# Attention and FFN on one core: the preparation of keys, values and weights rebuilt

## The reference

```python
kv = latent_kv @ Wkv_expand.T                      # ctx (8, 64, 256), Wkv (2048, 256)
k, v = jnp.split(kv, 2, axis=-1)
qp = q @ Wq.T                                      # q = layernorm(x), x (8, 1024, 1024)
scores = einsum(qh, kh) / sqrt(64)                 # 16 heads of 64, 64 keys; causal mask
attn = softmax(where(causal, scores, min))
x = x + einsum(attn, vh) @ Wout.T
# then, on layernorm(x): both sides rounded to fp8 (e4m3) by one scale each,
x = x + scaled_mm(x_fp8, w_fp8.T)
```

## Time and profile before

| | us |
|---|---|
| median of 3 runs | 1797.81 |
| lowest and highest run | 1797.55, 1800.09 |
| the profiled execution, its own time | 1799.89 |
| its span, first to last instruction | 1798.1 |
| TensorE busy | 1744.1 (97%) |
| VectorE busy | 1343.6 (75%) |
| ScalarE busy | 689.0 (38%) |
| GpSimd busy | 185.3 (10%) |
| HBM read, written | 119.28 MB, 71.30 MB |

### The profile page before, as it was taken

The page is one execution under the profiler, slowest core; times in us unless marked ns, Lnnn a source line. Parts: engine busy times, 40 slices in busy tenths (PEclk is TensorE's granted clock), DMA queues, the critical chain, the costliest instruction groups (busy, mean ns, idle before and its releaser), DMA issues.

```text
span 1798.1 us, 26754 instructions
## 1 busy us (share of the span) xinstructions
PE 1744.1 (97%) x10698; PEld 842.0 (47%) x10730; DVE 1343.6 (75%) x1844; ACT 689.0 (38%) x643; POOL 185.3 (10%) x143
## 2 busy tenths in 40 slices
PE   8689999999999999999999999999999999799998
PEld 4434454445444544454445444544454443455554
DVE  6776778677866787778777877787778665777776
ACT  5632133223322332233223322332233221788886
POOL 0000000000000000000000000000000011355555
PEclk9899999999999999999999999999999999899999
DMA  9664545454545354545454545454544444777763
GB/s 317 158 185 118 136 105 129 117 137 104 129 117 140 100 129 117 124 117 129 117 124 117 129 117 125 116 129 117 124 117 117 117 112 122 267 270 268 269 245 140
DMA packets 371689, 263.96 MB, mean 147 GB/s; under 512 B 322320, under 2 KB 324880, under 8 KB 371088
## 3 DMA queue, kind: packets, MB, share of 16 engines
q1 hardware_dynamic: 371600, 262.71, 53.7%
HBM read 119.28 MB, written 71.30 MB: 106 GB/s over the span
## 4 chain that ended last, share of the span: by engine, by line
PE 91%; issue 5%; DVE 2%; ACT 1%; DMA 1%; POOL 0%; SPq 0%; POOLq 0%; DVEq 0%
PE ps_all L623 70%; PE ps_all L760 12%; PE ps_all L610 2%; PE ps_all L632 2%; PE ps_all L596 1%; PE ps_all L597 1%; PE ps_all L693 1%; PE ps_all L575 1%; DVE n_buf L1066 1%; ACT tile_space L844 0%; ACT n_buf L832 0%; DMA tile_space<-tile_space 0%; DVE amax L1045 0%; DMA tile_space<-in_ctx_dram 0%; PE ps_all L565 0%
## 5 line engine op out<-in xcount | busy, mean ns | idle before, releaser
L623 PE MATMUL ps_all<-m_buf,tile_space 128*128 128x512 f16 x3072 | 681.6, 381 | 4.7 <-DVE wo_t L1267 4.7
L623 PE MATMUL ps_all<-n_buf,tile_space 128*128 128x512 f16 x3024 | 670.0, 379 | 0.0
L623 PEld LDWEIGHTS ps_all<-m_buf,tile_space 128*128 128x128 f16 x3072 | 298.5, 98 | 368.9 <-issue 13.1
L623 PEld LDWEIGHTS ps_all<-n_buf,tile_space 128*128 128x128 f16 x3024 | 292.1, 98 | 350.1 <-issue 6.2
L760 PE MATMUL ps_all<-wo_t,tile_space 128*128 128x512 bf16 x992 | 231.1, 381 | 2.8 <-DVE tile_space L1377 1.2
L858 ACT ACTIVATE tile_space<-tile_space,neg_mean 128x1024 f32<-128x1024 f32 x63 | 72.4, 1149 | 327.6 <-DVE neg_mean L1153 327.6
L514 POOL TENSOR_TENSOR rstd_x<-veps_x,minus_half 128x1 f32<-128x1 f32 x64 | 35.3, 551 | 1388.2 <-DVE veps_x L1096 1388.2
L854 ACT ACTIVATE tile_space<-tile_space,score_scale 128x1024 f32<-128x1024 f32 x64 | 73.5, 1148 | 230.9 <-DVE tile_space L1123 230.9
L760 PEld LDWEIGHTS ps_all<-wo_t,tile_space 128*128 128x128 bf16 x1024 | 97.8, 98 | 107.7 <-issue 1.7
L850 ACT ACTIVATE tile_space<-tile_space 128x1024 f16<-128x1024 f32 x64 | 67.6, 1057 | 184.5 <-DVE tile_space L1133 184.5
L1083 DVE SCALAR_TENSOR_TENSOR tile_space<-tile_space 128x1024 f16<-128x1024 f32 x64 | 78.4, 1225 | 64.0 <-ACT tile_space L850 64.0
(11 more groups left out here) (128 smaller groups left out, 1700.6 us busy)
## 6 DMA issues: line engine op xcount, KB each, us to landing
tile_space<-in_x_dram SPq DMA_DIRECT2D x128, 512.0 KB, 3.8
x_scratch<-tile_space SPq DMA_DIRECT2D x64, 512.0 KB, 3.0
m_buf<-x_scratch SPq DMA_DIRECT2D x32, 512.0 KB, 4.0
tile_space<-x_scratch SPq DMA_DIRECT2D x32, 512.0 KB, 4.0
out_dram<-m_buf SPq DMA_DIRECT2D x32, 512.0 KB, 2.9
out_dram<-tile_space SPq DMA_DIRECT2D x31, 512.0 KB, 2.9
m_buf<-in_L_xattn_Wq_dram SPq DMA_DIRECT2D x4, 1024.0 KB, 11.1
n_buf<-in_L_xattn_Wout_dram SPq DMA_DIRECT2D x2, 2048.0 KB, 18.3
```

Of the source, the lines that this page charges most:

```text
L623: mm = nc.tensor.matmul(to[:, cols], left[:, ls, c * P:(c + 1) * P], right[:, rs, c, cols], start=(c == 0 and i == 0), stop=(c == CT - 1 a ...
```

## The change

It rebuilds the preparation and leaves the steady steps as they are but for the order of the blocks of N (and with it of the columns of p) and for some transfers in batch 0.

- Keys and values are split straight from PSUM, without the f32 copy; their scales come from bounds made of the context's maximum and sums over Wkv, so they are there before the products.
- A maximum is taken across partitions by spreading it over 128 columns, a transpose on TensorE and a reduction on VectorE (`spread_peaks`, `turn_peaks`, `all_peaks`) in place of GpSimd's instruction.
- Wq is split in place inside `wq_stack`, unstacked. The first M is made of it by `first_m`, three passes of 64 rows deep, 48 matmuls of 64 columns a piece in place of 32; two pieces are made ahead, the other six between the chunks of the first score product.
- Wout isn't turned on TensorE: it is split as it lies (blocks 1, 3 and 5: low half by GpSimd), and SP turns the 8 blocks, high and low half together, by DMA transpose. All 8 must have landed before the first pair of N; three pairs of the first N stand in s(1), the last in o(0).
- What the later batches need is done within batch 0 by SP (`later`): the keys stored in step 1, three quarters of Wq stored in step 2 and loaded back stacked in steps 3 and 4; the keys of batch 1 are loaded in step 5 in place of step 0, the fp8 weight in step 6 in place of ahead of step 0.

```diff
+        w8_flat = w8_raw[:].rearrange("p j c -> p (j c)").bitcast(F16)
+        k_split = [w8_flat[:, i:i + 4096].rearrange("p (j k) -> p j k", k=KEYS) for i in (0, 4096)]
+        V_SLOTS = (9, 10, 11, 2)
+        v_split = [tile_space[:, i, :].bitcast(F16).rearrange("p (s j k) -> p s j k", s=2, k=KEYS) for i in V_SLOTS]
+        wq_nat = [wq_stack[:].rearrange("p (j e) c -> p e j c", e=2)[:, s] for s in (0, 1)]
...
+        ORDER0 = "soxsoxposxpos"
+        SLOTS0 = [(ps_s, ps_o, ps_x, ps_p)["soxp".index(k)] for k in ORDER0]
+        EARLIER0 = [max((m for m in range(n) if ORDER0[m] == ORDER0[n]), default=None) for n in range(13)]
+        KV_USES = (3, 4, 5, 6, 9, 10, 11, 12)
+        PEAKS_AT = 1
+        BY_POOL = (1, 3, 5)
...
+            def store_wq(i):
+                e, rows = ((0, ODD), (1, EVEN), (1, ODD))[i]
+                sp.dma_start(wq_dram[i], wq_heads(e)[rows]).then_inc(wq_out, 16)
+
+            def restack_wq(i):
+                e, rows = ((1, ODD), (0, ODD), (1, EVEN))[i]
+                sp.dma_start(wq_heads(e)[rows], wq_dram[i]).then_inc(wq_back, 16)
...
+            def first_v(g2):
+                part = slice(2 * g2, 2 * g2 + 2)
+                sp.wait_ge(kv_read, 5 + g2)
+                for s in range(2):
+                    sp.dma_start(v_rows[:, s, part, :], v_split[g2][:, s, :, 0:SK]).then_inc(got_v, 16)
+                for s in range(2):
+                    sp.dma_start(kv_dram[s, :, NP + 2 * g2:NP + 2 * g2 + 2, :], v_split[g2][:, s]).then_inc(kv_stored, 16)
+
+            def turn_wout(a):
+                lo_done(sp, a)
+                sp.dma_start_transpose(wo_blocks[:, :, a * P:(a + 1) * P], wout_split[a]).then_inc(wout_turned, 16)
+
             sp.wait_ge(x_lo, 1)
             turn_x(0, 0)
             load_x(xa, got_xa, 2, 0)
-            sp.wait_ge(kv_stored, 32)
+            for g2 in range(3):
+                first_v(g2)
+            sp.wait_ge(turned, 13)
+            turn_wout(0)
+            turn_wout(1)
+            first_v(3)
             sp.wait_ge(x_lo, 2)
             turn_x(1, 1)
             load_x(xa, got_xa, 3, 1)
-            sp.wait_ge(v_split, 1)
-            load_v(lambda s: (v_hi_t, v_lo_t)[s][:, :, 0:SK])
-            for s, src in enumerate((v_hi_t, v_lo_t)):
-                sp.dma_start(kv_dram[s, :, NP:NG, :], src).then_inc(kv_stored, 16)
+            for a in range(2, CT):
+                turn_wout(a)
+            sp.wait_ge(kv_stored, 128)
...
+            def later(tt):
+                if tt == 1:
+                    for k in range(2):
+                        sp.wait_ge(grow_full[k], QUAD)
+                    for s, src in enumerate(k_split):
+                        sp.dma_start(kv_dram[s, :, 0:NP, :], src).then_inc(k_stored, 16)
+                if tt == 2:
+                    for i in range(3):
+                        store_wq(i)
+                if tt == 3:
+                    sp.wait_ge(wq_out, 48)
+                    for i in range(2):
+                        restack_wq(i)
+                if tt == 4:
+                    restack_wq(2)
+                    sp.wait_ge(k_stored, 32)
+                if tt == 6:
+                    sp.dma_start(w8_raw[:], Wffn.rearrange("(a p) c -> p a c", p=P)).then_inc(got_w8, 16)
...
+                if is_step(tt, 5 if b == 0 else 0) and not (known and t >= T - TB):
...
+            def scale_wout(a):
+                nc.gpsimd.tensor_scalar(wout_f[:, a, :], wout_f[:, a, :], to_f16[:, 2:3], None,
+                                        ALU.mult).then_inc(wout_scaled, 1)
+
+            pool.wait_ge(scales_made, 4)
+            scale_wout(1)
+            for a in (1, 3, 5):
+                if a < 5:
+                    scale_wout(a + 2)
+                pool.wait_ge(wout_hi, a + 1)
+                nc.gpsimd.tensor_tensor(wout_split[a][:, H:2 * H], wout_f[:, a, :], wout_split[a][:, 0:H],
+                                        ALU.subtract).then_inc(wout_lo[1], 1)
...
+            def turn_peaks(i):
+                pe.wait_ge(peak_rows, i + 1)
+                for k in range(2 if i == 0 else 1):
+                    mm = nc.tensor.transpose(PEAK_PS[i][:, k * P:(k + 1) * P], peak_spread[i][:, k * P:(k + 1) * P], ident[:])
+                mm.then_inc(peak_turned, 1)
...
+            def first_m(ct):
+                to = grow_ps[ct % 2]
+                if ct >= 2:
+                    pe.wait_ge(grow_free[ct % 2], ct // 2)
+                for j in range(NP):
+                    for i, (ws, ks) in enumerate(PASSES):
+                        for k, rows in enumerate((EVEN, ODD)):
+                            cols = to[:, (k * NP + j) * SK:(k * NP + j + 1) * SK]
+                            mm = nc.tensor.matmul(cols, wq_nat[ws][rows, j, ct * P:(ct + 1) * P],
+                                                  k_split[ks][rows, j, 0:SK],
+                                                  start=(i == 0), stop=(i == len(PASSES) - 1))
+                mm.then_inc(grow_full[ct % 2], 1)
...
+                                if t == 0:
+                                    pe.wait_ge(wout_turned, 16 * CT)
...
+            pe.wait_ge(wq_split, 4)
+            pe.wait_ge(kv_read, 6)
+            for c in range(2):
+                first_m(c)
             pe.wait_ge(x_turned, 16)
-            split_product(ps_s, xt_buf[0], m_buf, s_full)
+            pe.wait_ge(kv_read, 8)
+
+            def first_chunk(c):
+                pe.wait_ge(grow_free[c % 2], c // 2 + 1)
+                if c + 2 < CT:
+                    first_m(c + 2)
+                if c == PEAKS_AT:
+                    turn_peaks(3)
+
+            split_product(ps_s, xt_buf[0], m_buf, s_full, ready=first_chunk)
...
+            act.wait_ge(scales_made, 4)
+            split_wout_hi(0)
             x_high(1, 1)
-
-            nc.scalar.activation(v_hi_t, v_f, ACT.Copy, scale=to_f16[:, 3:4]).then_inc(v_hi, 1)
+            for c in range(3, CT):
+                take_m(c, c // 2)
+                split_wout_hi(c - 2)
+            split_wout_hi(6)
+            split_wout_hi(7)
...
+            then(nc.vector.tensor_reduce(small[:, 15:16], peaks[:, 0:8], AX.X, ALU.max))
+            spread_peaks(3, small[:, 15:16])
+            variance(1, 1)
+            take_m(2, 1)
+            all_peaks(3, amax4_all[:, 2:3])
+            powers(slice(2, 3), 4)
             then(nc.vector.tensor_scalar(out_scale[:], from_f16[:, 2:3], from_f16[:, 3:4],
                                          1.0 / (N_SCALE * P_SCALE), ALU.mult, ALU.mult))
-            for c in range(CT):
-                take_m(c, c // 2)
-                take_wout(c)
-                if c == 2:
-                    variance(0, 0)
-                if c == 3:
-                    normalise(0, 0)
-                if c == 5:
-                    x_low(0, 0)
-            variance(1, 1)
             normalise(1, 1)
+            split_wout_lo(0)
+            take_m(3, 1)
             x_low(1, 1)
-            dve.wait_ge(v_hi, 1)
-            nc.vector.scalar_tensor_tensor(out=v_lo_t, in0=v_f, scalar=to_f16[:, 3:4], in1=v_hi_t, op0=ALU.mult,
-                                           op1=ALU.subtract).then_inc(v_split, 1)
-            dve.wait_ge(kv_stored, 32)
+            take_m(4, 2)
+            split_wout_lo(2)
+            take_m(5, 2)
+            split_wout_lo(4)
+            take_m(6, 3)
+            split_wout_lo(6)
+            take_m(7, 3)
+            split_wout_lo(7)
+
+            nc.vector.memset(wait_carrier[:], 0.0).then_inc(x1_ready, 1)
+            dve.wait_ge(kv_stored, 128)
```

430 lines of the change are left out of this document (238 added, 192 removed).

## The result

| | before | after |
|---|---|---|
| median | 1798.16 (8 runs) | 1802.95 (8 runs) |
| lowest and highest run | 1797.16, 1800.09 | 1799.84, 1805.28 |
| the profiled execution, its span | 1799.89, 1798.1 | 1803.8, 1802.0 |
| TensorE busy | 1744.1 | 1743.2 |
| VectorE busy | 1343.6 | 1348.6 |

The changed kernel is slower: ratio 1.0024, 95% interval 1.0013 to 1.0034, some 4 us. The forecast was 1792.8. The last two rows of the table tell where to look: at the end of o(0) the changed kernel is 8.0 us ahead, as forecast (8.6), and six steps later it is 3.3 us behind. The preparation won its time, and batch 0 gave back 11.2 us.

A forecast was written before the change was run, and what follows sets the result against it. TensorE was taken to bound the kernel, with VectorE and ScalarE setting when its rhythm starts. 8.6 us won in the preparation less 3.6 lost in batch 0 is 5.0, so 1797.81 becomes 1792.8 us; range 1785 to 1801.

The forecast's parts named there:

- What bounds the kernel: Whole kernel: TensorE, busy 97% of the span, 179.74 us per batch; before its rhythm it waits for VectorE and ScalarE.
- the mark: End of the first product with N, o(0), in batch 0: 120.2 us forecast against 128.8 before, 8.6 won.
- First, the scores: Preparation: VectorE's list reaches the fourth scale at 61.1 us, and the first scores end at 77.8, 15.0 earlier.
- Second, the turned Wout: Ahead of N's first pair: eight transposes of Wout land at 94.6 us, TensorE stands 5.1, o(0) ends at 120.2.
- 114.7: End of o(0) in us without the wait for turned Wout, if a turn takes 2.2 us or less.
- Third, batch 0: SP's queue in batch 0: three stores of Wq at 224 GB/s, 14.1 us, delay a turned x; 3.6 us lost once.
- one stall 3.6: Batch 0: TensorE waits 3.6 us, once, for a turned x behind the stores of Wq.
- S: Start of the next step in batch 0, 149.5 us for the first; stores forecast to last until S + 17.9.
- The sum: Whole kernel: 8.6 won less 3.6 lost, 5.0 us won, giving 1792.8 us; chance 0.37.
- the rivals: Whole kernel: no stall 1789.2 us (0.22), fast turns 1787.3 (0.12), turns by issue 1799.7 (0.19), no overlap 1813.4 (0.10).
- the two on the slow side: Wout's turns: spaced by issue, 3.77 us each, 1799.7 (chance 0.19); or not overlapping, 5.3 each, 1813.4 (chance 0.10).
- The price of a turn: One transpose of Wout behind another on SP's queue: 2.9 us forecast; rivals 1.3 (0.12), 3.77 (0.19), 5.3 (0.10).

The follow-up runs named there:

- experiment 2: The changed kernel, same bytes, with batch 0's transfers of Wq and keys spread, one of 1.05 MB per gap of SP's queue: 1790.84 us, ratio 0.9955 to before.
- the spread kernel: The kernel of experiment 2: the changed kernel with one transfer of 1.05 MB in each gap of SP's queue in batch 0; 1790.84 us.
- the load behind the turns: The spread kernel with the load of x(3) alone moved behind the eight turns of Wout: 1790.14 us, ratio 0.9952 to before.

## Why the prediction went wrong, step by step

- **What bounds the kernel, and the mark.** Right. After s(7) of batch 0 both kernels keep the same rhythm, and what the preparation changes shows nearly in full (experiment 2).
- **First, the scores.** The fourth scale was made at 60.2 (60.09 + 0.16), forecast 61.1: counting VectorE's list held over 55 us. The scores ended at 81.1, forecast 77.8. The term that was too small is that of the low halves behind the scale: the four of Wout ahead of the last piece of M took 8.5 us (1.27, 2.02, 3.17, 2.01), not some 4.8, and the normalisation 1.5, not 0.8. Rows of VectorE and GpSimd's beside them:

```profile
67.45 2.02 DVE L1161 SCALAR_TENSOR_TENSOR tile_space<-n_buf,to_f,tile_space 128x1024 f16<-128x1024 f32 x1
...
72.19 3.17 DVE L1161 SCALAR_TENSOR_TENSOR n_buf<-n_buf,to_f 128x1024 f16<-128x1024 f32 x1 [1.58 <-ACT n_buf L910]
75.28 1.21 DVE L1174 SCALAR_TENSOR_TENSOR m_buf<-ps_all,m_buf 128x1024 f16<-128x1024 f32 x1
```

```profile
68.37 3.81 POOL L561 TENSOR_SCALAR n_buf<-n_buf,to_f 128x1024 f32<-128x1024 f32 x1
72.15 5.19 POOL L570 TENSOR_TENSOR n_buf<-n_buf 128x1024 f16<-128x1024 f32 x2
```

- **Second, the turned Wout.** All landed at 95.46, forecast 94.6. The last five turns stood 2.3 to 2.6 us apart in the queue, forecast 2.9; the values' part took 3.7 us of the queue where I had 1.1, and the last turn landed 2.0 us behind the end of its issue, not 0.5. The errors cancel, which is luck. So is the start at 68.5 (68.4 measured): my 67.2 for block 1's low half was 1.2 too early, and no term of mine leads from it to 68.5. The wait was 3.4 for 5.1, since the scores were later. From the landing to the mark 25.2 us, forecast 25.5. So the mark came out: 120.7 for 120.2. That 0.1 us a turn is worth 0.8 at the mark did not hold all the way. From the end of the first scores to the mark I had 42.4 us with a wait of 5.1 and 36.9 without one. Measured are 39.6 with 3.4 (the change), 38.0 with 2.0 (the spread kernel) and 37.5 with 0.35 (the load behind the turns). So the first 1.4 us of wait were worth 1.6 at the mark, the next 1.7 only 0.5, since VectorE's order then ends next; with that changed too it is 36.6. No kernel has the scores at 77.8, so none could show 114.7.
- **Third, batch 0: the step that failed.** I had "one stall 3.6". The mechanism was the one forecast, in its place, but three terms were missing or too small.
  - *The stall itself* was 6.55. The stores ended at 183.6 (the third, issued near 165.9, plus 17.7), which is S + 21.5, not S + 17.9. I had given them the queue alone at 224 GB/s for 14.1 us; they landed 7.2, 11.2 and 17.7 us after their issues at 164.5, 165.2 and 165.9, so 4.7 us apart and then 7.2. The 7.2 us at the 223 GB/s of that stretch are 1.6 MB, more than the third store's 1.05, and the store of x1 landed 2.5 us behind it: so I read it that the two moved together, which no run tried. Taken away by itself in the kernel before, it was worth 6.1 us, not 4.7.
  - *The half clock behind it*: 2.79. I had read a wait of 4.07 with a clock of 0.56 behind it, used it for the preparation, and did not carry it to my own stall, which was 3.6 by my count.
  - *The second wait*: 1.90 (behind it the clock stayed). I had named the keys' loads of step 5 in the change and never costed them; they stand in SP's order ahead of the turn of x(7), behind a load of Wq of 64 partitions.
- **The sum**: won 8.0 and not 8.6, lost 11.2 and not 3.6, so 3.3 lost at s(7) where 5.0 were to be won. Of the rivals none had it: the two on the slow side priced a turn at 3.77 or 5.3, and took the stall as I did.
- **The price of a turn.** It was 2.3 to 2.6 us behind another one; the 2.9 taken from the earlier trace rows was too high (the row itself, 4.5 us less 1.29, gives 3.2 and not the 2.8 to 3.1 I wrote), and neither 1.3 nor 3.77 nor 5.3 came true. (The rate of the Trainium skill, "DMA: Bandwidth & Descriptors", section "Latency and other measured facts", gave an estimated 2.0, which is as near as the row, from the other side.)

## What to carry to other kernels

A transfer that nobody waits for still costs what it puts ahead of the next one that somebody does: before adding it to an ordered queue, find the queue's gaps, and give each gap one piece that fits (here 1.05 MB between two turns), with all partitions in it where the layout allows. When a stall is forecast, price what follows from it as well: the clock behind it, and the next transfers that now stand closer together. And where a wait at a resource is the last to end, ask whose order ends next, since removing it may buy only the difference.

## What the runs showed of the hardware

- With three stores of 1.05 MB in the queue, it moved 222 GB/s when they were of 64 partitions and 426 when they were of 128 (176 to 180 us, DMA shares 0.97 and 1.02).
- The issue of a transpose took 3.3 us with a load of x ahead, and with stores of Wq of 64 partitions ahead as well 5.8 (one), 9.8 (two) and 14.1 (three); with three of 128 partitions it was 6.4. The issue on SP's queue stretches with what is ahead and how slowly it moves, so a long issue in these profiles marks a full queue and not a costly instruction.
- The product behind a wait of 6.4 to 6.9 us took 1.5 to 2.8 us longer, at mean clocks of 0.78 to 0.87; what stood behind waits of 0.53, 0.80, 1.73 and 2.50 us took nothing more.
- VectorE's low halves of Wout, with two large operands in SBUF, took 2.02, 3.17 and 2.01 us in place of 1.27 when a `tensor_tensor` of GpSimd was running as they began, and each ended 1.1 us after that one had; those with one operand in PSUM took 1.21 as ever. In the kernel with the load behind the turns one low half began 0.07 us ahead of such a `tensor_tensor` (70.93 and 71.00): there it took 1.29, and GpSimd's 3.20 in place of 2.13. So of these pairs the one that began second was late; no run took GpSimd's part away. (The Trainium skill, "Advanced Engine Details and Errata", section "GPSIMD Details", says that GpSimd shares an interface with VectorE and conflicts with its instructions that have two SBUF inputs; the rows agree, but for two: the low half of Wout at 61.93 took 1.27 and that of x at 65.19 took 1.21, both beside a `tensor_scalar` of GpSimd.)
